# Experts stage of a decoder layer: results and row numbers in four buffers, each with its own semaphore, instead of two

## The chip, the core and the metric

The kernel runs on one core of one Trainium2 chip. The metric is the device time of one execution in microseconds (us), as the median of several runs.

## What is computed

One decoder layer over 32 batches of 100 tokens of width 256, all in fp32: self-attention (16 heads of 64), cross-attention to 361 context rows per batch (16 heads of 16), and a mixture of experts. Only the last part is touched. Its reference, cut down (`feats` is the layer-normed input of the stage, 3200 rows of 256; E is 8, the inner width is 1024):

```python
aff = feats @ centroids.T
eid = jnp.argmax(aff, axis=1)
xhat = (feats - mu) * jax.lax.rsqrt(var + EPS)
for e in range(E):
    mask = (eid == e).astype(feats.dtype)[:, None]
    h = xhat * gamma[e] + beta[e]
    y = feats + jax.nn.relu(h @ w1[e] + b1[e]) @ w2[e] + b2[e]
    alpha = jax.nn.sigmoid(feats @ centroids[e])[:, None]
    out = out + mask * (alpha * y + (1.0 - alpha) * feats)
x = x + out
```

Every token goes to one expert, so `out` plus the residual is, per row, `xf + alpha * (relu(h @ w1 + b1) @ w2 + b2)`, with `xf` the input row plus its normed features.

## The kernel before

Self-attention and cross-attention take about the first 1200 us of the program. During cross-attention each token's row is also written, sorted by expert, into the DRAM tensor `routed_rows` (`xs`), with the token's number as its 257th word. Then `experts` (L2002) works through 20 tiles, written out one after the other in the program, in the repeated pattern of `HALVES` = 2, 2, 1, 2, 1: a tile with 2 halves has 256 rows (a big tile, twelve of them), a tile with 1 half has 128 (a small tile, eight of them). The small tiles are tiles 2, 4, 7, 9, 12, 14, 17 and 19. Which expert and which rows belong to a tile is read from a table at run time (`expert_of`, `load_rows`).

What each engine does, in the order of its own program:

- SP loads, for tile j + 2, the rows (L1993, three buffers) and then 2 MB of weights `w1` and `w2` (L1998, L1999, three buffers). The rows wait for tile j - 1's `xf` (on POOL) and its `token` (on DVE, semaphore `token_ready`, L2072); the weights wait for the last `psd_y` of tile j - 1.
- TensorE multiplies `h_in` by `w1` into four banks `psd_h` (L2249: eight groups f = 0 to 7; in fp32 each group is four matmuls in the trace). Group f waits until group f - 4 has been copied out of its bank (`copied`, L2247). Then it multiplies `hid` by `w2` into `psd_y` (L2260: per half, 16 matmuls in the trace), and transposes the next tile's `xhat` in between (L2229).
- ScalarE copies groups 0, 2, 4, 6 and 7 to `hid` with bias and relu (L2143), then scales the next tile's transposed rows to `h_in` (L2129) and computes `ez` = exp(-z) (L2133).
- VectorE (DVE) copies groups 1, 3 and 5 to `hid` (L2201). Between group 1 and group 3 it takes the moments of the next tile (L2155, L2159), and after group 5 it runs `normalize(j + 1)` (`xhat` L2166, `feats` L2171) and `weigh(j + 1)`: the product with the centroid (L2179), its sum `z` (L2183), the row numbers `token` (L2185), then `ez` + 1 (L2187, after ScalarE's exp) and `alpha` (L2190). Only then comes tile j's own end: `y` = `psd_y` + bias (L2215) and `res` (L2219), for each half. All of it is one queue: what stands behind `token` in this order waits with it.
- GpSimd (POOL) runs `roots(j + 1)` (L2083 to L2087), then `finish(j - 1)`, which issues one indirect DMA per half that scatters `res` to the output rows that `token` names (L2102), then `residual(j + 1)` (`xf`, L2095).

`token` and `res` have two buffers each, j % 2, and so has the semaphore `scattered` that counts their scatters. So DVE waits before it overwrites them:

```python
reach(dve, scattered[j % 2], 16 * halves_until(j, 2))
dve.tensor_copy(token[:, j % 2, 0:nh], rows[:, j % 3, 0:nh, D]).then_inc(token_ready, 1)
```

Here, in `weigh(j)`, the scatters of tile j - 2 must have landed. The same wait stands a second time before `y` and `res` of tile j (L2211), where it has already been met.

Of the kernel before, what the change touches and what calls it, by code (L numbers as in the profile page):

```python
# [2001 lines left out]
def experts(nc, c, xs, w1, w2, out):  # L2002
# [4 lines left out]
    with ExitStack() as ctx:  # L2007
# [21 lines left out]
        ez = sb("ez", [128, 2])  # L2029
        alpha = sb("alpha", [128, 2, 2])  # L2030
        xf = sb("xf", [128, 2, 2, D])
        token = sb("token", [128, 2, 2], U32)
        h_in = sb("h_in", [128, 2, KD, T])
        hid = sb("hid", [128, NF, T])
        y = sb("y", [128, 2, D])
        res = sb("res", [128, 2, 2, D])

        ps_x = psum("psd_x", [128, KD * T])
        ps_h = [psum(f"psd_h{i}", [128, 512]) for i in range(4)]
# [10 lines left out]
        ez_ready = sem("ez_ready")  # L2050
        weight_steps = sem("weight_steps")
        xf_ready = sem("xf_ready")
        token_ready = sem("token_ready")
        turned = sem("turned4")
        h_in_ready = sem("h_in_ready")
        hid_filled = sem("hid_filled")
# [9 lines left out]
        @block.sync  # L2066
        def _(sp):
            load_rows(sp, c, 1, xs)
            sp.wait_ge(c.tiles_ready, 4)
            for j in range(TILES - 2):  # L2070
                reach(sp, xf_ready, j)
                reach(sp, token_ready, j)  # L2072
                load_rows(sp, c, j + 2, xs)
                reach(sp, y_filled, halves_until(j))
                load_weights(sp, c, j + 2, w1_sb[(j + 2) % 3], w2_sb[(j + 2) % 3], w1, w2)

        @block.gpsimd
        def _(pool):
            def roots(j):
                nh = HALVES[j]  # L2080
                pool.wait_ge(moment_steps, 2 * halves_until(j + 1))
                pool.sem_inc(pool_passed, 1)
                pool.tensor_scalar(var_eps[:, 0, 0:nh], mv[:, 0:nh, 1], 1.0 + EPS, EPS * EPS, ALU.mult, ALU.add  # L2083
                                   ).then_inc(root_steps, 1)
                pool.tensor_scalar(var_eps[:, 1, 0:nh], mv[:, 0:nh, 1], EPS, None, ALU.add).then_inc(root_steps, 1)
                pool.wait_ge(root_steps, 3 * j + 2)
                pool.tensor_tensor(rstd[:, :, 0:nh], var_eps[:, :, 0:nh],  # L2087
                                   c.minus_half[:, 0:2 * nh].rearrange("p (u t) -> p u t", u=2), ALU.pow
                                   ).then_inc(root_steps, 1)

            def residual(j):
                nh = HALVES[j]
                pool.wait_ge(normalised, 2 * j + 2)
                reach(pool, res_ready, halves_until(j - 1))
                pool.tensor_tensor(xf[:, j % 2, 0:nh], rows[:, j % 3, 0:nh, 0:D], feats[:, 0:nh], ALU.add  # L2095
                                   ).then_inc(xf_ready, 1)

            def finish(j):
                for t in range(HALVES[j]):
                    pool.wait_ge(res_ready, halves_until(j) + t + 1)  # L2100
                    pool.sem_inc(pool_passed, 1)
                    pool.indirect_dma_start(  # L2102
                        out=out, out_offset=bass.IndirectOffsetOnAxis(ap=token[:, j % 2, t:t + 1], axis=0),
                        in_=res[:, j % 2, t, :], in_offset=None, bounds_check=B * S - 1,
                        oob_is_err=False).then_inc(scattered[j % 2], 16)

            roots(0)
            residual(0)
            for j in range(TILES):
                if j + 1 < TILES:  # L2110
                    roots(j + 1)
                if j > 0:
                    finish(j - 1)
                if j + 1 < TILES:
                    residual(j + 1)
            finish(TILES - 1)
            for j in (TILES - 2, TILES - 1):
                pool.wait_ge(scattered[j % 2], 16 * halves_until(j + 2, 2))

        @block.scalar  # L2120
        def _(act):
# [26 lines left out]
        @block.vector  # L2148
        def _(dve):
            dve.wait_ge(c.tables, 16 * 5)  # L2150

            def moments(j):
                dve.wait_ge(rows_loaded[j % 3], 16 * (j // 3 + 1))
                for t in range(HALVES[j]):
                    dve.bn_stats(stats[:, t], rows[:, j % 3, t, 0:D]).then_inc(moment_steps, 1)  # L2155
                dve.wait_ge(moment_steps, halves_until(j) + halves_until(j + 1))
                dve.sem_inc(dve_passed, 1)
                for t in range(HALVES[j]):
                    dve.bn_aggr(mv[:, t], stats[:, t]).then_inc(moment_steps, 1)  # L2159

            def normalize(j):

                dve.wait_ge(root_steps, 3 * j + 3)
                reach(dve, turned, j)
                for t in range(HALVES[j]):
                    ins = dve.tensor_scalar(xhat[:, t], rows[:, j % 3, t, 0:D], mv[:, t, 0:1], rstd[:, 0, t:t + 1],  # L2166
                                            ALU.subtract, ALU.mult)
                ins.then_inc(normalised, 1)
                reach(dve, xf_ready, j)
                for t in range(HALVES[j]):  # L2170
                    ins = dve.tensor_scalar(feats[:, t], rows[:, j % 3, t, 0:D], mv[:, t, 0:1], rstd[:, 1, t:t + 1],  # L2171
                                            ALU.subtract, ALU.mult)
                ins.then_inc(normalised, 1)

            def weigh(j):
                nh, e = HALVES[j], expert_of(dve, c, j)
                dve.wait_ge(normalised, 2 * j + 2)
                dve.sem_inc(dve_passed, 1)
                dve.tensor_tensor(prod[:, 0:nh], feats[:, 0:nh], c.cen[:, bass.ds(e, 1), :].to_broadcast([128, nh, D]),  # L2179
                                  ALU.mult).then_inc(weight_steps, 1)  # L2180
                dve.wait_ge(weight_steps, 3 * j + 1)
                reach(dve, ez_ready, j)
                dve.tensor_reduce(z[:, 0:nh], prod[:, 0:nh], AX_X, ALU.add).then_inc(z_ready, 1)  # L2183
                reach(dve, scattered[j % 2], 16 * halves_until(j, 2))
                dve.tensor_copy(token[:, j % 2, 0:nh], rows[:, j % 3, 0:nh, D]).then_inc(token_ready, 1)  # L2185
                dve.wait_ge(ez_ready, j + 1)
                dve.tensor_scalar(ez[:, 0:nh], ez[:, 0:nh], 1.0, None, ALU.add).then_inc(weight_steps, 1)  # L2187
                dve.wait_ge(weight_steps, 3 * j + 2)
                reach(dve, res_ready, halves_until(j - 1))
                dve.reciprocal(alpha[:, j % 2, 0:nh], ez[:, 0:nh]).then_inc(weight_steps, 1)  # L2190

            moments(0)
            normalize(0)
            weigh(0)
            for j in range(TILES):
                nh, e = HALVES[j], expert_of(dve, c, j)
                for f in HID_DVE:
                    dve.wait_ge(hid_filled, NF * j + (f + 1))
                    if f == 1:
                        reach(dve, y_filled, halves_until(j))  # L2200
                    dve.tensor_scalar(hid[:, f, 0:UNIT * nh], ps_h[f % 4][:, 0:UNIT * nh], c.b1_sb[:, f, bass.ds(e, 1)],  # L2201
                                      0.0, ALU.add, ALU.max).then_inc(hid_dve, 1)
                    if f == 1 and j + 1 < TILES:
                        moments(j + 1)
                if j + 1 < TILES:
                    normalize(j + 1)
                    weigh(j + 1)
                e = expert_of(dve, c, j)
                dve.wait_ge(weight_steps, 3 * j + 3)
                dve.wait_ge(xf_ready, j + 1)  # L2210
                reach(dve, scattered[j % 2], 16 * halves_until(j, 2))  # L2211
                for t in range(nh):
                    n = halves_until(j) + t
                    dve.wait_ge(y_filled, n + 1)
                    dve.tensor_tensor(y[:, t], ps_y[n % 3][:, 0:D], c.b2_sb[:, bass.ds(e, 1), :].rearrange(  # L2215
                        "p o d -> p (o d)"), ALU.add).then_inc(y_ready, 1)
                for t in range(nh):
                    dve.wait_ge(y_ready, halves_until(j) + t + 1)
                    dve.scalar_tensor_tensor(out=res[:, j % 2, t], in0=y[:, t], scalar=alpha[:, j % 2, t:t + 1],  # L2219
                                             in1=xf[:, j % 2, t], op0=ALU.mult, op1=ALU.add).then_inc(res_ready, 1)  # L2220

        @block.tensor
# [44 lines left out]
def build(nc, ins, out):  # L2267
    c = Shared()
    with ExitStack() as ctx:
# [16 lines left out]
        c.tiles_ready = ctx.enter_context(nc.semaphore("tiles_ready"))  # L2286
        c.empty = sb("empty", [128, ROWW])
        c.xs_cleared = ctx.enter_context(nc.semaphore("xs_cleared"))
        c.scattered = [ctx.enter_context(nc.semaphore(f"scattered{p}")) for p in range(2)]
        c.act_passed = ctx.enter_context(nc.semaphore("act_passed"))  # L2290
        c.dve_passed = ctx.enter_context(nc.semaphore("dve_passed"))
        c.pool_passed = ctx.enter_context(nc.semaphore("pool_passed"))
# [61 lines left out]
```

## Time and profile before

| | |
|---|---|
| median of 3 runs | 1494.63 us (1489.18, 1494.63, 1497.31) |
| profiled execution, its own time | 1491.62 us |
| its span | 1489.4 us, so 2.2 us lie around it |
| TensorE busy | 1374.4 us (92%) |
| VectorE busy | 939.5 us (63%) |
| ScalarE busy | 759.9 us (51%) |
| GpSimd busy | 652.3 us (44%) |
| experts stage, first to last of TensorE's steady work | 1254.3 to 1482.2 us |

Busy shares are means over stages of the program with different limits. In the rows further on, PE is TensorE, ACT is ScalarE, POOL is GpSimd, and "idle before" is the time an engine stood still just before an instruction, with the instruction that ended it behind the arrow.

### The profile page before, as it was taken

Reading aid. Unit: us, or ns where it says so; the run is one execution under the profiler, and the core shown is the slowest. Engines: PE = TensorE matmul, PEld = TensorE weight load, DVE = VectorE, ACT = ScalarE, POOL = GpSimd, SP = SyncE. Lnnn points to the kernel's source line nnn. Section 1 sums busy time; section 2 is a strip of 40 time slices with the busy share of each in tenths; the row PEclk is TensorE's granted clock in tenths of the full one; section 3 lists DMA queues with packets and bytes.
Section 4 is the critical chain, followed back from the end, with each engine's and each line's share of the span. In section 5 each row is a group of like instructions: output and inputs, shape, how many; then the busy total and the mean of one; then the engine's idle time right before and its main releaser. Section 6 shows DMA issues by size and latency. Waiting matters only on the chain.

```text
span 1489.4 us, 39019 instructions
## 1 busy us (share of the span) xinstructions
PE 1374.4 (92%) x12161; PEld 1188.1 (80%) x12161; DVE 939.5 (63%) x2386; ACT 759.9 (51%) x1880; POOL 652.3 (44%) x1000
## 2 busy tenths in 40 slices
PE   6999999999999999869999999999999947999997
PEld 5888888887878787757888888888888836887886
DVE  6757574747484756446777777777777754555453
ACT  5747474646465655515665656566565522222222
POOL 5635344443526271722345555545555442333332
PEclk9999999999999999979999999999999978999999
DMA  6607161524344343547677667776676626655551
GB/s 203 145 1 172 25 151 43 130 64 111 83 90 104 76 118 68 130 135 193 186 187 199 189 174 195 193 191 182 185 193 188 181 70 213 214 202 189 201 198 69
DMA packets 181115, 217.42 MB, mean 146 GB/s; under 512 B 83486, under 2 KB 148933, under 8 KB 180774
## 3 DMA queue, kind: packets, MB, share of 16 engines
q1 hardware_dynamic: 176424, 209.60, 51.2%
q0 software_dynamic: 3584, 6.58, 1.4%
q8 instruction: 43, 0.70, 0.2%
q10 hardware_dynamic: 1024, 0.21, 0.1%
q14 instruction: 40, 0.33, 0.1%
HBM read 137.62 MB, written 79.43 MB: 146 GB/s over the span
## 4 chain that ended last, share of the span: by engine, by line
PE 44%; DVE 4%; DMA 3%; issue 3%; POOL 2%; DVEq 0%; SPq 0%; ACT 0%; POOLq 0%; ACTq 0%
PE psb_s L1769 7%; PE psd_y L2260 6%; PE psb_o L1792 5%; PE psb_t L1779 5%; PE psd_h L2249 5%; PE psb_p L62 4%; PE psb_p L63 3%; PE psb_p L64 3%; DMA out<-res,token 2%; PE psb_p L1732 2%; PE psb_f L1815 2%; DVE row_max L1488 1%; PE psb_f L1800 1%; PE psb_p L1827 1%; PE psb_f L1806 1%
## 5 line engine op out<-in xcount | busy, mean ns | idle before, releaser
L1488 DVE TENSOR_REDUCE row_max<-psb_s 100x1 f32<-100x361 f32 x512 | 265.5, 531 | 142.1 <-PE psb_s L1769 136.2
L1362 ACT ACTIVATE probs<-psb_t 121x400 f32<-121x400 f32 (+1 forms) x384 | 190.5, 508 | 87.6 <-PE psb_t L1779 81.4
L1769 PE MATMUL psb_s<-k,q 97*100 97x362 f32 x512 | 185.2, 364 | 14.1 <-DMA k<-packed_keys 5.4
L540 POOL TENSOR_TENSOR diag<-neg_ident,row_max 100x400 fp32r<-100x400 f32 x128 | 112.9, 903 | 168.8 <-DVE row_max L632 140.1
L1779 PE MATMUL psb_t<-q,k 98*121 98x200 f32 (+1 forms) x768 | 146.3, 273 | 1.7 <-ACT probs L1362 1.7
L1779 PEld LDWEIGHTS psb_t<-q,k 98*121 98x121 f32 (+1 forms) x768 | 125.3, 184 | 4.6 <-ACT probs L1362 2.4
L451 ACT ACTIVATE probs<-ps_t 100x400 f32<-100x400 f32 x128 | 57.5, 501 | 111.5 <-PE ps_t L787 111.5
L1769 PEld LDWEIGHTS psb_s<-k,q 97*100 97x100 f32 x512 | 85.8, 168 | 34.0 <-issue 20.7
L2143 ACT ACTIVATE hid<-psd_h,b_sb 128x256 f32<-128x256 f32 (+1 forms) x100 | 43.2, 432 | 121.0 <-PE psd_h L2249 120.9
L2249 PE MATMUL psd_h<-h_in,w_sb 128*128 128x256 f32 (+1 forms) x448 | 86.7, 350 | 8.4 <-DVE hid L2201 6.9
L1792 PE MATMUL psb_o<-probs,v_ext 121*32 121x100 f32 (+1 forms) x3072 | 92.7, 253 | 0.0
L526 POOL CAST o_hi<-stage 128x400 fp32r<-128x400 f32 x64 | 59.9, 936 | 69.5 <-ACT stage L461 33.4
L2249 PEld LDWEIGHTS psd_h<-h_in,w_sb 128*128 128x128 f32 x448 | 74.7, 194 | 19.4 <-DVE hid L2201 9.2
L306 ACT COPY q_t<-ps_p 64x200 f32<-64x200 f32 x112 | 57.1, 510 | 63.4 <-PE ps_p L64 62.5
L62 PE MATMUL ps_p<-x_lo,w_hi 128*128 128x400 f32 x224 | 82.1, 366 | 4.6 <-DVE q_t L306 0.2
L632 DVE TENSOR_REDUCE row_max<-ps_s 100x4 f32<-100x400 f32 x128 | 67.6, 571 | 28.6 <-PE ps_s L743 28.1
L461 ACT COPY stage<-ps_ot 64x200 f32<-64x200 f32 x256 | 81.8, 319 | 6.1 <-PE ps_ot L797 1.2
L528 POOL TENSOR_TENSOR o_lo<-stage,o_hi 128x400 fp32r<-128x400 f32 x64 | 81.8, 1277 | 5.1
L2260 PE MATMUL psd_y<-w_sb,hid 128*128 128x256 f32 x368 | 83.9, 379 | 0.0
L1792 PEld LDWEIGHTS psb_o<-probs,v_ext 121*32 121x32 f32 (+1 forms) x3072 | 64.4, 110 | 21.3 <-issue 16.9
L64 PE MATMUL ps_p<-x_hi,w_hi 128*128 128x400 f32 x224 | 77.2, 345 | 0.0
L63 PE MATMUL ps_p<-x_hi,w_lo 128*128 128x400 f32 x224 | 76.7, 342 | 0.0
(252 smaller groups left out, 3714.3 us busy)
## 6 DMA issues: line engine op xcount, KB each, us to landing
w_sb<-in_w SPq DMA_DIRECT2D x28, 1024.0 KB
routed_rows<-empty SPq DMA_DIRECT2D x7, 3855.0 KB, 19.6
packed_keys<-k_st SPq DMA_DIRECT2D x32, 724.0 KB, 4.2
k<-packed_keys SPq DMA_DIRECT2D x64, 362.0 KB
v_rows<-v_tok SPq DMA_DIRECT2D x32, 400.0 KB
v_ext<-v_rows SPq DMA_DIRECT2D x32, 400.0 KB
q<-packed_queries SPq DMA_DIRECT2D x64, 200.0 KB
w_third<-in_w SPq DMA_DIRECT2D x12, 1024.0 KB
```

Source lines behind the costliest of these rows:

```text
L62: pe.matmul(out, hi_l, lo_r, start=first, stop=False)
L63: pe.matmul(out, lo_l, hi_r, start=False, stop=False)
L64: return pe.matmul(out, hi_l, hi_r, start=False, stop=last)
L461: act.copy(*turned_part(r - 2, a, odd)).then_inc(ot_copied_act, 1)
L540: pool.tensor_tensor(diag[:, g % 2], c.neg_ident[0:S, 0:S].unsqueeze(1).to_broadcast([S, GH, S]), row_max[:, g // 2 % 2, g % 2].unsqueeze( ...
L1362: act.activation(probs[0:KT[kt], u % 2, kt], ps_t[i % 2][0:KT[kt], 0:4 * S], ACT.Exp, scale=HD2 ** -0.5).then_inc(probs_ready, 1)
L1488: dve.reduce_max(row_max[:, p, h:h + 1], ps_s[h % 2][0:S, 0:S2], AX_X).then_inc(max_ready, 1)
L1769: pe.matmul(ps_s[h % 2][0:S, 0:S2E], q2[0:97, p, u, g, S * a:S * (a + 1)], k2[0:97, p, u, g], start=True, stop=True).then_inc(scores_ready, 1)
L1779: ins = pe.matmul(ps_t[i % 2][0:n, 2 * S * g:2 * S * (g + 1)], k2[:, p, u, g, rows], q2[:, p, u, g], start=True, stop=True)
L1792: ins = pe.matmul(ps_o[32 * h:32 * (h + 1), S * u:S * (u + 1)], v_ext[0:n, p, kt, 4 * u + h, :], probs[0:n, u % 2, kt, S * h:S * (h + 1)], ...
L2249: ins = pe.matmul(ps_h[f % 4][:, 0:UNIT * nh], w1_sb[j % 3][:, k, 128 * f:128 * (f + 1)], h_in[:, j % 2, k, 0:UNIT * nh], start=(k == 0), ...
L2260: ins = pe.matmul(ps_y[n % 3][:, 0:D], hid[:, f, UNIT * t:UNIT * (t + 1)], w2_sb[j % 3][:, f, :], start=(f == 0), stop=(f == NF - 1))
```

## The change

`token` and `res` get four buffers, j % 4, and `scattered` becomes four semaphores, so that tile j waits for the scatters of tile j - 4. `token_ready` is gone: `token` now counts on `weight_steps`, which takes four steps per tile instead of three, and SP waits there for the same instruction as before. The end of the stage waits for the last four tiles' scatters instead of the last two. No instruction is added, taken away or moved on any engine; only what some of them wait for differs.

```diff
-        token = sb("token", [128, 2, 2], U32)
+        token = sb("token", [128, 4, 2], U32)
...
-        res = sb("res", [128, 2, 2, D])
+        res = sb("res", [128, 4, 2, D])
...
-        token_ready = sem("token_ready")
...
-                reach(sp, token_ready, j)
+                reach(sp, weight_steps, 4 * (j - 1) + 2)
...
-                        out=out, out_offset=bass.IndirectOffsetOnAxis(ap=token[:, j % 2, t:t + 1], axis=0),
-                        in_=res[:, j % 2, t, :], in_offset=None, bounds_check=B * S - 1,
-                        oob_is_err=False).then_inc(scattered[j % 2], 16)
+                        out=out, out_offset=bass.IndirectOffsetOnAxis(ap=token[:, j % 4, t:t + 1], axis=0),
+                        in_=res[:, j % 4, t, :], in_offset=None, bounds_check=B * S - 1,
+                        oob_is_err=False).then_inc(scattered[j % 4], 16)
...
-            for j in (TILES - 2, TILES - 1):
-                pool.wait_ge(scattered[j % 2], 16 * halves_until(j + 2, 2))
+            for j in range(TILES - 4, TILES):
+                pool.wait_ge(scattered[j % 4], 16 * halves_until(j + 4, 4))
...
-                dve.wait_ge(weight_steps, 3 * j + 1)
+                dve.wait_ge(weight_steps, 4 * j + 1)
                 reach(dve, ez_ready, j)
                 dve.tensor_reduce(z[:, 0:nh], prod[:, 0:nh], AX_X, ALU.add).then_inc(z_ready, 1)
-                reach(dve, scattered[j % 2], 16 * halves_until(j, 2))
-                dve.tensor_copy(token[:, j % 2, 0:nh], rows[:, j % 3, 0:nh, D]).then_inc(token_ready, 1)
+                reach(dve, scattered[j % 4], 16 * halves_until(j, 4))
+                dve.tensor_copy(token[:, j % 4, 0:nh], rows[:, j % 3, 0:nh, D]).then_inc(weight_steps, 1)
                 dve.wait_ge(ez_ready, j + 1)
                 dve.tensor_scalar(ez[:, 0:nh], ez[:, 0:nh], 1.0, None, ALU.add).then_inc(weight_steps, 1)
-                dve.wait_ge(weight_steps, 3 * j + 2)
+                dve.wait_ge(weight_steps, 4 * j + 3)
...
-                dve.wait_ge(weight_steps, 3 * j + 3)
+                dve.wait_ge(weight_steps, 4 * j + 4)
                 dve.wait_ge(xf_ready, j + 1)
-                reach(dve, scattered[j % 2], 16 * halves_until(j, 2))
+                reach(dve, scattered[j % 4], 16 * halves_until(j, 4))
...
-                    dve.scalar_tensor_tensor(out=res[:, j % 2, t], in0=y[:, t], scalar=alpha[:, j % 2, t:t + 1],
+                    dve.scalar_tensor_tensor(out=res[:, j % 4, t], in0=y[:, t], scalar=alpha[:, j % 2, t:t + 1],
...
-        c.scattered = [ctx.enter_context(nc.semaphore(f"scattered{p}")) for p in range(2)]
+        c.scattered = [ctx.enter_context(nc.semaphore(f"scattered{p}")) for p in range(4)]
```

## Rows read from the trace of the kernel before

**Rows 1.** The page, busy time, share of the span and instructions of each engine.
```profile
PE 1374.4 (92%) x12161; PEld 1188.1 (80%) x12161; DVE 939.5 (63%) x2386; ACT 759.9 (51%) x1880; POOL 652.3 (44%) x1000
```

**Rows 2.** Stretches: busy time by engine, granted TensorE clock, DMA share, GB/s.
```profile
750.00:810.00 60.00, 59.34 (x695) 51.33 (x695) 43.73 (x119) 36.12 (x97) 29.30 (x55) 1.00 0.68 180
1237.00:1254.30 17.30, 16.41 (x69) 14.16 (x70) 8.24 (x22) 4.44 (x11) 2.85 (x5) 0.85 0.40 138
1254.30:1482.20 227.90, 218.64 (x1145) 191.13 (x1143) 117.90 (x320) 59.91 (x149) 76.63 (x103) 1.00 0.55 186
```

**Rows 3.** TensorE's waits from 1254 to 1483 us: total, times, longest.
```profile
PE psd_h L2249 <- DVE hid L2201: 9.1, 7, 1.9
```

**Rows 4.** VectorE's longest waits, same stretch and columns.
```profile
DVE token L2185 <- DMA out<-res,token: 27.8, 15, 3.2
DVE ez L2187 <- ACT ez L2133: 19.4, 11, 2.9
```

**Rows 5.** TensorE in order of time: start, duration, operation, idle before, at tiles 1, 2, 3, 10.
```profile
1254.30 7.07 PE L2249 MATMUL psd_h<-h_in,w_sb 128*128 128x256 f32 x32
1261.20 3.62 PE L2260 MATMUL psd_y<-w_sb,hid 128*128 128x256 f32 x16
...
1268.33 3.95 PE L2249 MATMUL psd_h<-h_in,w_third 128*128 128x128 f32 x32
...
1276.13 4.48 PE L2249 MATMUL psd_h<-h_in,w_sb 128*128 128x256 f32 x20
1281.98 2.86 PE L2249 MATMUL psd_h<-h_in,w_sb 128*128 128x256 f32 x12 [1.38 <-DVE hid L2201]
1284.68 3.62 PE L2260 MATMUL psd_y<-w_sb,hid 128*128 128x256 f32 x16
...
1360.32 4.48 PE L2249 MATMUL psd_h<-h_in,w_sb 128*128 128x256 f32 x20
1366.66 2.86 PE L2249 MATMUL psd_h<-h_in,w_sb 128*128 128x256 f32 x12 [1.86 <-DVE hid L2201]
1369.36 3.62 PE L2260 MATMUL psd_y<-w_sb,hid 128*128 128x256 f32 x16
```

**Rows 6.** VectorE in order of time, from tile 3's weights to its first copy.
```profile
1275.55 0.69 DVE L2183 TENSOR_REDUCE z<-prod 128x2 f32<-128x512 f32 x1
1278.96 0.17 DVE L2185 CAST token<-stage 128x2 uint32<-128x2 f32 x1 [2.72 <-DMA out<-res,token]
1279.03 0.16 DVE L2187 TENSOR_SCALAR ez<-ez 128x2 f32<-128x2 f32 x1
1279.23 0.17 DVE L2190 RECIPROCAL alpha<-ez 128x2 f32<-128x2 f32 x1
1280.15 0.42 DVE L2215 TENSOR_TENSOR y<-psd_y,b_sb 128x256 f32<-128x256 f32 x1 [0.75 <-DVE alpha L2190]
1280.61 0.48 DVE L2219 SCALAR_TENSOR_TENSOR res<-y,alpha,xf 128x256 f32<-128x256 f32 x1
1281.45 0.48 DVE L2201 TENSOR_SCALAR hid<-psd_h,b_sb 128x256 f32<-128x256 f32 x1 [0.35 <-issue]
```

**Rows 7.** The chain of waits, start, duration, what.
```profile
1274.79 4.14 DMA out<-res,token
```

**Rows 8.** POOL in order of time, behind that transfer's issue.
```profile
1275.78 1.30 POOL L2095 TENSOR_TENSOR xf<-stage,feats 128x512 f32<-128x512 f32 x1
```

**Rows 9.** VectorE in order of time at tile 0, with no scatter to wait for.
```profile
1237.90 0.69 DVE L2183 TENSOR_REDUCE z<-prod 128x2 f32<-128x512 f32 x1
1238.50 0.16 DVE L2185 CAST token<-stage 128x2 uint32<-128x2 f32 x1
1238.86 0.17 DVE L2187 TENSOR_SCALAR ez<-ez 128x2 f32<-128x2 f32 x1 [0.20 <-ACT ez L2133]
```

**Rows 10.** ScalarE in order of time, tile 3's exponential.
```profile
1276.27 0.20 ACT L2133 ACTIVATE ez<-z 128x2 f32<-128x2 f32 x1 [0.47 <-DVE z L2183]
```

**Rows 11.** VectorE in order of time, the longest product with the centroid (tile 6).
```profile
1309.40 1.66 DVE L2179 TENSOR_TENSOR prod<-feats,cen 128x512 f32<-128x512 f32 x1 [0.24 <-DVE feats L2171]
```

## Prediction

> **What bounds the kernel now.** The page comes first: TensorE is busy 92% of the span [rows 1], so a change pays only where it shortens TensorE's work or one of its pauses. Second, the stretches: from 1254.3 to 1482.2 us, where tiles 1 to 19 run, TensorE is busy 218.64 of 227.90 us at a granted clock of 1.00 [rows 2]. That leaves 9.26 us of pause, the most visible prize in the part of the program that the diff touches. Third, who TensorE waited for there: one partner alone, VectorE's copy `hid`, 7 times, 9.1 us, at most 1.9 each [rows 3]. Fourth, who VectorE waited for: `token` for the scatters, 27.8 us in 15 waits, then `ez` for ScalarE, 19.4 us in 11 [rows 4]. So the 27.8 us are not what can be won. The question is how much of them reaches TensorE.
>
> The timeline at tile 3 shows how they do. Tile 2 is small, so TensorE is through it in 7.8 us (1268.33 to 1276.13) [rows 5]. VectorE has summed `z` at 1275.55 to 1276.24 and could write `token` at once. It does so at 1278.96 [rows 6], when the second scatter of tile 1, issued at 1274.79, has landed 4.14 us later [rows 7]. Behind `token` in VectorE's queue stand `ez`, `alpha`, tile 2's `y` and `res`, and only then group 1 of tile 3, at 1281.45 [rows 6]. TensorE needs that bank for group 5 and stops until 1281.98 [rows 5]. The same picture comes at every big tile that follows a small one: tiles 3, 5, 8, 10, 13, 15, 18. The other eight of the 15 waits are followed by a wait for `ez`, which comes from ScalarE and in the end from TensorE, so they are covered and worth nothing.
>
> **What the change removes.** Tile 1, big and behind a big tile, shows an undisturbed first half: from the first `psd_h` matmul to the first `psd_y` one, 1261.20 − 1254.30 = 6.90 us for 32 matmuls, 0.216 us each. Tile 3 needs 1284.68 − 1276.13 = 8.55 us, 1.65 more, although its listed pause is 1.38; tile 10 needs 1369.36 − 1360.32 = 9.04, 2.14 more, with 1.86 listed [rows 5]. So a stop costs about 0.27 us beyond the idle shown, as the pipeline refills. Seven stops: 9.1 + 7 × 0.27 = **11.0 us**.
>
> Does VectorE come early enough without the wait? Tile 0 has no scatter to wait for: `token` starts 0.60 us and `ez` + 1 starts 0.96 us after `z` starts [rows 9]. At tile 3 that puts `ez` + 1 at 1276.51, right behind ScalarE's exponential, which ends at 1276.47 [rows 10]. Before, it stood at 1279.03, so all behind it moves up by 2.52 us: `alpha` to 1276.71, `y` to 1277.63, `res` to 1278.09, group 1's copy to 1278.93. TensorE went on 0.53 us after that copy started (1281.45 to 1281.98), so bank 1 is free at 1279.46. TensorE arrives for group 5 at 1276.13 + 20 × 0.216 = 1280.44. The slack is 1.0 us, and the stop is gone, not shortened. The start of `z` lies 0.58 us ahead of TensorE's first `psd_h` matmul here; that sequence hangs on TensorE's own work, so the other six tiles should have the same slack. Group 3's copy follows with only the next tile's moments in between, is needed two groups later, and moves up with it.
>
> **What it adds.** Nothing on any queue: every engine issues the same instructions in the same order. The new wait of tile j is for tile j − 4's scatters. They are issued while tile j − 3 runs, about two tiles before (one small and one big, 7.8 + 14.0 us, at the least), and take some 4 us [rows 7]: 0. SP waits for the same `token` instruction under another semaphore's name, and its row loads start up to 2.8 us earlier; they were never late after tile 0: 0. POOL's last wait names four tiles instead of two, and the two older ones landed long before the last scatter: 0. The same bytes move in 11 us less, which lifts the DMA share from 0.55 to 0.55 × 227.9 / 216.9 = 0.58, while 0.68 stood beside undisturbed matmuls earlier [rows 2]: 0. The cover of all these zeros is TensorE's work of 7.8 us or more per tile. If it went, the next late thing would be group 1's copy, 1.0 us away, and then POOL's path to `xhat` in the small tiles.
>
> The cost that no row settles is how VectorE fares when its small operations run beside POOL's `xf`. At tile 3 `xf` runs from 1275.78 to 1277.08 [rows 8], and `token`, `ez` and `alpha` would now fall inside it; before, they came after it. The lower bound is nothing: `z`, 0.69 us here, runs into `xf` and takes the same 0.69 as at tile 0 [rows 6, 9]. The upper bound from rows is the product with the centroid at tile 6, 1.66 us beside `xf` [rows 11] against the 0.69 that `z` takes for as many elements, so 0.97 us on the path, just inside the slack of 1.0. I take nothing, since `z` is the nearest row in time and place; even the upper bound leaves the stop at about zero. What could shift beyond is kept in a rival.
>
> The Trainium skill ("SBUF — State Buffer", "SBUF: two separate sides") has a rule against this change: VectorE and GpSimd share a pair of ports as an exclusive lock, held for the whole instruction, and a VectorE copy, cast or tensor_scalar in a two-port mode is blocked until GpSimd is through. By that rule `ez` + 1 would wait for `xf`'s end at 1277.08 instead of starting at 1276.51; the slack would be 0.4 us instead of 1.0, and the sum still 11.0. No run here shows `token` or `ez` beside `xf`.
>
> **The sum.** Against the profiled execution's own time: 1491.62 − 11.0 = 1480.6 us. That execution lies 3.0 us below the median shown; the mean of all four times is 1493.2, and I take that as the base: 1493.2 − 11.0 = **1482.1 us**, 0.74% less. About 0.5% (7.5 us) is what a measurement of this kernel can tell from no change.
>
> **The rivals.**
>
> *Part of the stop stays.* `xf` and the small operations hold each other up by more than the slack, say 1.8 us instead of 0 to 0.97. For it: at tile 6 `xf` and the product overlap and one of them took over twice its time. Against it: `z` did not suffer. It would bring back 0.8 of idle at each of the seven tiles, with the refill 7 × (0.8 + 0.12) = 6.4 us: a gain of 4.6 us, 1488.6 us. Chance 0.06.
>
> *The change does not do what it says, or the wait is another's.* The releaser of `token` is inferred from semaphores; were it VectorE's own queue or the row buffer, the four buffers would free nothing. For it: nothing but that inference. Against it: the wait ends with the landing each time, and tile 0, which has no scatter to wait for, shows none. 1493.2 us. Chance 0.05.
>
> *Slower: TensorE's clock.* Without pauses TensorE would work about 217 us on end in this stage. If the granted clock then fell from its upper level (2.4 GHz) to its lower (1.2 GHz), each us of matmuls would cost two. The place is the tail of the stage; the deciding point is 11.0 us of matmuls at the lower level, less than one big tile (14.0 us). Two big tiles would give −11.0 + 28.0 = +17.0, 1510.2 us. For it: the clock was 0.85 in tile 0. Against it: that followed a long idle at the stage's opening, and from 750 to 810 us TensorE was busy 59.34 of 60 us at 1.00 [rows 2]. Chance 0.03.
>
> **How the numbers follow.** The forecast has 0.86. Within it I give 0.08 to a measurement that comes out within 0.5%, because 11.0 us is only 3.5 above that bound and runs of one kernel spread over 8 us. Faster: 0.86 − 0.08 = 0.78. Same: 0.08 + 0.06 + 0.05 = 0.19. Slower: 0.03. The range takes the run spread around the forecast, 1489.18 − 11.0 = 1478.2 at the fast end with 1.5 us to spare, so 1476.7, and reaches up over the partial case to 1489.0. The no-change case and the slow one, 0.08 together, lie outside.
>
> **What would show it.** In the new profile TensorE's waits for `hid` in this stage are gone, and each of the seven segments from `psd_h` to `psd_y` is 6.9 us. The wait of `token` for the DMA is gone in all 15 places; `ez` takes over part of it in the eight covered ones, so VectorE's wait for ScalarE grows by several us, at no cost. Group 1's copy at tile 3 starts 2.8 us after TensorE's first `psd_h` matmul instead of 5.3. The stretch from tile 1 to tile 19 shrinks from 227.9 to 217 us with TensorE busy 99% or more of it, clock 1.00. I would be wrong if stops of 0.3 us or more remain at these tiles, if a wait for POOL (`xhat`, `xf`) appears in their place, or if the clock row falls.

## The result and the profile after

The changed kernel takes 1483.57 us (median of 6 runs, 1481.74 to 1484.26), the kernel before, run beside it, 1495.12 us. The ratio is 0.9926, 95% interval 0.9909 to 0.9942: 0.74% or 11.0 us less by the ratio, and 11.55 us between the two medians.

The page's line on engines, which answers to [rows 1]:

```profile
PE 1375.4 (93%) x12161; PEld 1191.5 (80%) x12161; DVE 943.5 (64%) x2386; ACT 760.0 (51%) x1880; POOL 651.0 (44%) x1000
```

TensorE does the same instructions in the same busy time; VectorE is busy 4.0 us longer, which comes up again below. The stretch from tile 1's first `psd_h` to the end of tile 19's `psd_y` answers to the third line of [rows 2]:

```profile
1256.24:1472.94 216.70, 216.69 (x1145) 191.71 (x1143) 122.05 (x320) 59.90 (x149) 76.20 (x103) 1.00 0.58 196
```

It lasted 227.85 us before (1254.30 to 1482.15) and lasts 216.70 us now: 11.15 us less. TensorE is busy 216.69 of them, at a granted clock of 1.00. In this stretch the view of waits, which had [rows 3] for TensorE, has no line for TensorE's matmuls at all. The span fell from 1489.4 to 1480.3 us, 9.1; the other 2 us are the stages ahead, where this execution reached the stage 1.9 us later (1256.24 against 1254.30).

TensorE in order of time at tiles 2, 3 and 10 (start, duration, operation), against [rows 5]:

```profile
1270.28 3.95 PE L2248 MATMUL psd_h<-h_in,w_third 128*128 128x128 f32 x32
...
1278.07 7.07 PE L2248 MATMUL psd_h<-h_in,w_sb 128*128 128x256 f32 x32
1284.98 3.62 PE L2259 MATMUL psd_y<-w_sb,hid 128*128 128x256 f32 x16
...
1357.76 7.07 PE L2248 MATMUL psd_h<-h_in,w_sb 128*128 128x256 f32 x32
1364.66 3.62 PE L2259 MATMUL psd_y<-w_sb,hid 128*128 128x256 f32 x16
```

Tile 3's 32 matmuls are one piece again, 1284.98 − 1278.07 = 6.91 us instead of 8.55, and tile 10's 6.90 instead of 9.04. Over the seven tiles the segments lost 10.98 us of the stretch's 11.15; most of the rest is tile 7, small, whose segment took 3.77 us instead of 3.91.

VectorE's waits in the stretch (total, times, longest), against [rows 4]:

```profile
DVE ez L2186 <- ACT ez L2132: 32.0, 11, 3.8
DVE hid L2200 <- PE psd_h L2248: 15.0, 23, 1.2
```

The wait of `token` for the scatters, 27.8 us in 15 times, is gone. The wait for ScalarE's exponential grew from 19.4 to 32.0 us at no cost. Of these 12.6 us, 11.3 stand at the eight tiles where `token` had been covered, and there 9.2 us of its wait are gone: mostly the same idle time under another name.

VectorE in order of time at tile 3, against [rows 6], and POOL's `xf` beside it:

```profile
1277.49 0.69 DVE L2182 TENSOR_REDUCE z<-prod 128x2 f32<-128x512 f32 x1
1278.09 0.95 DVE L2184 CAST token<-stage 128x2 uint32<-128x2 f32 x1
1278.96 0.15 DVE L2186 TENSOR_SCALAR ez<-ez 128x2 f32<-128x2 f32 x1
1279.15 0.17 DVE L2189 RECIPROCAL alpha<-ez 128x2 f32<-128x2 f32 x1
1280.00 0.42 DVE L2214 TENSOR_TENSOR y<-psd_y,b_sb 128x256 f32<-128x256 f32 x1 [0.69 <-DVE alpha L2189]
1280.46 0.48 DVE L2218 SCALAR_TENSOR_TENSOR res<-y,alpha,xf 128x256 f32<-128x256 f32 x1
1281.30 0.48 DVE L2200 TENSOR_SCALAR hid<-psd_h,b_sb 128x256 f32<-128x256 f32 x1 [0.35 <-issue]
```

```profile
1277.72 1.29 POOL L2094 TENSOR_TENSOR xf<-stage,feats 128x512 f32<-128x512 f32 x1
```

`token` now follows `z` without a gap, but lasts 0.95 us instead of 0.16: it ends at 1279.04, when `xf` ends at 1279.01. Group 1's copy starts 1281.30 − 1278.07 = 3.23 us after TensorE's first `psd_h` matmul, against 5.32 before and the 2.80 that the prediction worked out.

A way to read all the runs below follows from this. Call that distance d: from TensorE's first `psd_h` matmul of a tile to VectorE's copy of group 1. [rows 5] and [rows 6] suggest that the copy may start up to d = 3.78 us without harm: TensorE arrives for group 5 after 20 matmuls, 4.31 us, and it went on 0.53 us after the copy started. The lengths of the segments put this limit a little lower, at 3.68 us (table below, under "How much slack there is"), and by it the slack is 3.68 − d. Before, d was 5.32 at tile 3 and the slack −1.64; now it is +0.45. Over the seven tiles d now lies between 3.08 and 3.30, so the slack is 0.38 to 0.60 us.

### The profile page after: what moved, and what is told of

Same layout as the page of the kernel before. It is cut to its first block, busy times and chain, and to the rows that moved or that the text cites. A ratio compares the mean times of both kernels' runs of the same rounds, so it can differ in the third digit from the quotient of the medians.

```text
span 1480.3 us, 39018 instructions
## 1 busy us (share of the span) xinstructions
PE 1375.4 (93%) x12161; PEld 1191.5 (80%) x12161; DVE 943.5 (64%) x2386; ACT 760.0 (51%) x1880; POOL 651.0 (44%) x1000
## 4 chain that ended last, share of the span: by engine, by line
PE 46%; DVE 4%; issue 2%; DMA 2%; POOL 1%; SPq 1%; ACT 0%; DVEq 0%; ACTq 0%; POOLq 0%
PE psd_h L2248 8%; PE psd_y L2259 7%; PE psb_s L1769 6%; PE psb_t L1779 4%; PE psb_o L1792 4%; PE psb_p L62 4%; PE psb_p L63 3%; PE psb_p L64 3%; DVE row_max L1488 2%; PE psb_p L1732 2%; PE psb_f L1815 2%; DVE k_st L1471 1%; PE psb_f L1800 1%; DMA k<-packed_keys 1%; PE psb_p L1827 1%
```

## The experiments

A profile's span also holds the stages ahead, which differ from one execution to the next (tile 1 began anywhere from 1254 to 1268 us). So for mechanisms I compare the stretch from tile 1 to tile 19 in each profile, and the timed ratio to the kernel before for the whole.

**Which of the buffers matters.** Two kernels take the change apart. The first keeps two buffers of results and two semaphores:

```diff
-        res = sb("res", [128, 4, 2, D])
+        res = sb("res", [128, 2, 2, D])
...
-                reach(dve, scattered[j % 4], 16 * halves_until(j, 4))
                 dve.tensor_copy(token[:, j % 4, 0:nh], rows[:, j % 3, 0:nh, D]).then_inc(weight_steps, 1)
...
-                reach(dve, scattered[j % 4], 16 * halves_until(j, 4))
+                reach(dve, scattered[j % 2], 16 * halves_until(j, 2))
```

> Four buffers of row numbers, but two of results and two semaphores as before; the row numbers wait for nothing of their own, since VectorE waits for the scatters of tile j - 4 before it writes tile j - 2's results. Theory A (the stop comes from the row numbers' wait alone, because it stands ahead of y, res and group 1's copy): all of the gain, ratio about 0.993 to the kernel before, no wait of TensorE for hid, span near 1480 us. Rival B (the wait for two result buffers, met today only because the other wait comes first, becomes the new stop): VectorE waits for the scatter at y, up to 2.7 us at the seven places less the 2 us that pass between the two instructions, so stops of 0.3 to 1 us stay and the ratio is 0.995 to 1.0.

Measured: ratio 0.9908 (0.9882 to 0.9934), stretch 216.83 us, no wait of TensorE for `hid`. Theory A holds: the wait in front of `y` is met when VectorE gets there. The reason is in the program. `token` of tile j + 1 is written while tile j runs, ahead of tile j's own `res`. So with two buffers it waits for the scatters of tile j − 1, which have only just been issued, while `res` of tile j waits for those of tile j − 2, a whole tile older. The expected span of about 1480 us did not come: this execution spent longer in the stages ahead, reached tile 1 at 1265.65 us and had a span of 1489.8.

The second has four buffers of results only:

```diff
-        res = sb("res", [128, 2, 2, D])
+        res = sb("res", [128, 4, 2, D])
...
-                        in_=res[:, j % 2, t, :], in_offset=None, bounds_check=B * S - 1,
+                        in_=res[:, j % 4, t, :], in_offset=None, bounds_check=B * S - 1,
```

> Four buffers of results, but two of row numbers, with the waits of the kernel before. Theory A: nothing moves, ratio 1.000 within 0.002, the wait of token for the scatter 27 to 28 us in 15 times, TensorE waits for hid 7 times, 9 us. Rival B: a gain of a few us.

Measured: ratio 0.9998 (0.9980 to 1.0016), stretch 226.99 us. TensorE's and VectorE's waits from 1225 us on:

```profile
PE psd_h L2249 <- DVE hid L2201: 8.3, 7, 2.1
```

```profile
DVE token L2185 <- DMA out<-res,token: 27.1, 15, 3.5
```

Nothing moved. This edit changes no wait, only where `res` lies, so by itself it says little; together with the first kernel it says that the whole gain comes from `token`, 8 bytes per partition and buffer, and none from the 4 KB per partition that `res` took besides.

**How many buffers.** Both with three instead of four:

```diff
-        token = sb("token", [128, 4, 2], U32)
+        token = sb("token", [128, 3, 2], U32)
...
-        res = sb("res", [128, 4, 2, D])
+        res = sb("res", [128, 3, 2, D])
...
-                reach(dve, scattered[j % 4], 16 * halves_until(j, 4))
+                reach(dve, scattered[j % 3], 16 * halves_until(j, 3))
```

> Three buffers of both and three semaphores instead of four. The row numbers of tile j wait for tile j - 3's scatters, which land a whole tile (7.8 us or more) before. Theory A: same time as with four, ratio 0.993, no wait for the DMA at token. Rival (scatters run late enough that three are short): waits of token for the DMA of more than 0.2 us in some tiles and a ratio nearer 1.

Measured: ratio 0.9920 (0.9892 to 0.9947), stretch 216.72 us, no wait of `token` for the DMA. Three do what four do: with three, `token` too waits for scatters that are a tile older.

**Or no buffer more.** The kernel before, with the wait and the cast moved behind `res` in VectorE's queue (`number` holds the two lines that `weigh` loses; `number(0)` follows `weigh(0)`):

```diff
                 dve.tensor_reduce(z[:, 0:nh], prod[:, 0:nh], AX_X, ALU.add).then_inc(z_ready, 1)
-                reach(dve, scattered[j % 2], 16 * halves_until(j, 2))
-                dve.tensor_copy(token[:, j % 2, 0:nh], rows[:, j % 3, 0:nh, D]).then_inc(token_ready, 1)
...
                                              in1=xf[:, j % 2, t], op0=ALU.mult, op1=ALU.add).then_inc(res_ready, 1)
+                if j + 1 < TILES:
+                    number(j + 1)
```

> The kernel before with two buffers of each; the row numbers and their wait are moved from the weights of tile j + 1 to behind the results of tile j, so that y, res no longer stand behind the wait, but group 1's copy still does. Theory A (place in the queue is what counts; group 1's copy may start up to 3.78 us after the first psd_h matmul): at tile 3 the scatter lands 2.8 us after that matmul, so the copy starts at about 3.3 us and TensorE doesn't stop; at tile 10, where the landing came latest (3.3 us), the copy starts near 3.8 us, at the edge. All or nearly all of the gain: ratio 0.993 to 0.994. Rival (buffers are needed, the order doesn't matter): ratio 0.998 to 1.0, TensorE's seven waits stay.

Measured: ratio 0.9926 (0.9899 to 0.9953), stretch 217.76 us, 1.0 more than with four buffers. One of TensorE's seven waits is left in the view, at tile 10, the one expected at the edge:

```profile
1368.28 2.86 PE L2255 MATMUL psd_h<-h_in,w_sb 128*128 128x256 f32 x12 [0.23 <-DVE hid L2205]
```

VectorE there, with the wait for the scatter now behind `res`:

```profile
1365.76 0.49 DVE L2223 SCALAR_TENSOR_TENSOR res<-y,alpha,xf 128x256 f32<-128x256 f32 x1
1366.91 0.17 DVE L2193 CAST token<-stage 128x2 uint32<-128x2 f32 x1 [0.66 <-DMA out<-res,token]
1367.74 0.48 DVE L2205 TENSOR_SCALAR hid<-psd_h,b_sb 128x256 f32<-128x256 f32 x1 [0.67 <-PE psd_h L2255]
```

`psd_h` began at 1363.57, so d = 4.17, past 3.68 by 0.49; the segment is 0.49 us longer than 6.91, and 0.23 of that is shown as idle. The copy came later than the expected 3.8, since 0.66 us pass between the end of the cast and the copy. At tiles 8, 13 and 18 d was 3.77, 3.79 and 3.88, and the segments are 0.10, 0.11 and 0.20 us longer with no idle shown at all. Tile 18, whose segment is 1465.26 − 1458.15 = 7.11 us:

```profile
1458.15 7.27 PE L2255 MATMUL psd_h<-h_in,w_sb 128*128 128x256 f32 x32
1465.26 3.62 PE L2266 MATMUL psd_y<-w_sb,hid 128*128 128x256 f32 x16
```

Together these four are 0.90 of the 1.06 us that the stretch is longer. It was the order of VectorE's queue that turned a late scatter into a stop. The extra buffers are one cure, another order nearly as good a one.

**Why `token` lasts 0.95 us.** The changed kernel with the cast ahead of the product (the counts that wait on it shift by one):

```diff
+                reach(dve, scattered[j % 4], 16 * halves_until(j, 4))
+                dve.tensor_copy(token[:, j % 4, 0:nh], rows[:, j % 3, 0:nh, D]).then_inc(weight_steps, 1)
                 dve.tensor_tensor(prod[:, 0:nh], feats[:, 0:nh], c.cen[:, bass.ds(e, 1), :].to_broadcast([128, nh, D]),
                                   ALU.mult).then_inc(weight_steps, 1)
...
                 dve.tensor_reduce(z[:, 0:nh], prod[:, 0:nh], AX_X, ALU.add).then_inc(z_ready, 1)
-                reach(dve, scattered[j % 4], 16 * halves_until(j, 4))
-                dve.tensor_copy(token[:, j % 4, 0:nh], rows[:, j % 3, 0:nh, D]).then_inc(weight_steps, 1)
```

> The changed kernel with the row numbers written ahead of the product with the centroid, so that they no longer fall beside POOL's xf at the small tiles. Theory A (lock: what VectorE does as a copy, cast or tensor_scalar beside xf is held until xf ends): the 20 casts take 0.14 to 0.17 us each, but at small tiles ez + 1 takes their place, lasts 0.6 us or more instead of 0.15 and ends with xf; group 1's copy at tile 3 still starts 3.1 to 3.3 us after the first psd_h matmul. Rival B (only the conversion to an integer is slow there): ez + 1 lasts 0.16 us and group 1's copy starts 2.8 us after. The time is that of the changed kernel either way, ratio to the kernel before 0.992 to 0.993, since TensorE doesn't wait for it.

Measured: ratio 0.9925 (0.9902 to 0.9948), stretch 216.70 us. VectorE at tile 3, and POOL:

```profile
1278.08 0.17 DVE L2179 CAST token<-stage 128x2 uint32<-128x2 f32 x1
1278.20 0.69 DVE L2180 TENSOR_TENSOR prod<-feats,cen 128x512 f32<-128x512 f32 x1
1278.93 0.69 DVE L2184 TENSOR_REDUCE z<-prod 128x2 f32<-128x512 f32 x1
1279.88 0.58 DVE L2186 TENSOR_SCALAR ez<-ez 128x2 f32<-128x2 f32 x1 [0.27 <-ACT ez L2132]
```

```profile
1279.13 1.29 POOL L2094 TENSOR_TENSOR xf<-stage,feats 128x512 f32<-128x512 f32 x1
```

The cast here takes 0.17 us, and `ez` + 1, 0.15 us in the changed kernel, takes 0.58 and ends at 1280.46 with `xf` (1280.42). Over the seven tiles `ez` + 1 takes 0.39 to 0.58 us, a little under the 0.6 expected. d is 1282.65 − 1279.49 = 3.16, close to the 3.23 with the cast behind: theory A at this place. One part of the expectation failed. Over all 20 tiles the casts took 8.2 us, as much as in the changed kernel, and not 0.14 to 0.17 us each. At the five other big tiles, 0, 1, 6, 11 and 16, POOL starts `xf` before VectorE reaches the early cast, and there it is now the cast that is held, for 1.04 to 1.23 us. At tile 6, VectorE and then POOL:

```profile
1309.51 1.23 DVE L2179 CAST token<-stage 128x2 uint32<-128x2 f32 x1
```

```profile
1309.45 1.26 POOL L2094 TENSOR_TENSOR xf<-stage,feats 128x512 f32<-128x512 f32 x1 [0.18 <-DVE feats L2170]
```

In the changed kernel, as in the one before [rows 11], it is the product that is held at these tiles. At tile 6 of the kernel before, `xf` had started 0.15 us ahead of it:

```profile
1309.25 1.25 POOL L2095 TENSOR_TENSOR xf<-stage,feats 128x512 f32<-128x512 f32 x1 [0.19 <-DVE feats L2171]
```

The product took 1.66 us and ended 0.56 after `xf`. With the cast ahead, it starts once `xf` is through and takes 0.68:

```profile
1310.65 0.68 DVE L2180 TENSOR_TENSOR prod<-feats,cen 128x512 f32<-128x512 f32 x1
```

So whatever of these comes second beside `xf` pays. Moving an operation away from `xf` at one kind of tile put it beside `xf` at another.

**How much slack there is.** The changed kernel with one, then three sums between `y` and `res` of the seven small tiles that a big one follows; their results go nowhere (shown with three):

```diff
+                if nh == 1 and j + 1 < TILES:
+                    for n in range(3):
+                        dve.tensor_reduce(spare[:, n, 0:2], prod[:, 0:2], AX_X, ALU.add)
```

> The changed kernel with one more sum of 512 elements (0.60 us from start to start; its result goes nowhere) on VectorE between y and res of the seven small tiles that a big one follows. Theory A (slack of 0.5 to 0.6 us behind the held cast, then each further us costs seven): group 1's copy starts near 3.8 to 3.9 us, stops of 0 to 0.2 us, cost 0 to 2.5 us in all, ratio to the kernel before 0.993 to 0.995. Rival (slack of 1.0 us, as if the cast cost nothing): no listed stop at any of the seven, ratio 0.9925 or less. Rival (any delay of VectorE there is paid in full): 4.2 us, 0.996.

Measured: ratio 0.9930 (0.9902 to 0.9957), stretch 216.84 us, no stop. But this doesn't measure the slack: group 1's copy hardly moved, d = 3.26 instead of the expected 3.8 to 3.9. VectorE at tile 3:

```profile
1292.25 0.68 DVE L2219 TENSOR_REDUCE spare<-prod 128x2 f32<-128x512 f32 x1
1292.85 0.47 DVE L2222 SCALAR_TENSOR_TENSOR res<-y,alpha,xf 128x256 f32<-128x256 f32 x1
1293.24 0.48 DVE L2201 TENSOR_SCALAR hid<-psd_h,b_sb 128x256 f32<-128x256 f32 x1
```

The sum takes up 0.60 us of the queue, yet the copy moved by 0.03. The copy now starts 0.39 us after `res` instead of 0.84, and the 0.35 us of idle in that gap is gone; the sum starts 0.34 after `y` where `res` started 0.46 after it. The profile names no cause for that idle time ("issue"). The program has VectorE read the tile's expert number from a table at this place, and the reading that this work now goes on while the sum runs fits, but is not shown.

> The same with three such sums, 1.8 us. Theory A: group 1's copy starts 5.0 to 5.1 us after the first psd_h matmul (3.23 + 1.8), bank 1 is free 0.53 us later, TensorE arrives at 4.31: seven listed stops of 0.9 to 1.2 us and, with the refill, 7 x 1.3 = 9 us on top of the changed kernel's time, ratio to the kernel before 0.998 to 1.0. Rival (the gain came from elsewhere, for instance from DMA traffic or the row loads): the gain stays, ratio 0.993.

Measured: ratio 0.9967 (0.9949 to 0.9985), stretch 222.32 us, 5.6 more than the changed kernel. VectorE and TensorE at tile 3:

```profile
1279.51 1.86 DVE L2219 TENSOR_REDUCE spare<-prod 128x2 f32<-128x512 f32 x3
1281.29 0.47 DVE L2222 SCALAR_TENSOR_TENSOR res<-y,alpha,xf 128x256 f32<-128x256 f32 x1
1281.68 0.48 DVE L2201 TENSOR_SCALAR hid<-psd_h,b_sb 128x256 f32<-128x256 f32 x1
```

```profile
1277.24 4.48 PE L2252 MATMUL psd_h<-h_in,w_sb 128*128 128x256 f32 x20
1282.21 2.86 PE L2252 MATMUL psd_h<-h_in,w_sb 128*128 128x256 f32 x12 [0.49 <-DVE hid L2201]
1284.90 3.62 PE L2263 MATMUL psd_y<-w_sb,hid 128*128 128x256 f32 x16
```

d is 1281.68 − 1277.24 = 4.44, not the expected 5.0, since the first of the sums is all but free, as above. The segment takes 7.66 us instead of 6.91: 0.75 more. The seven segments together are 5.3 of the measured 5.6 us longer. The cost is less than the 9 us expected, and the ratio lies below the 0.998 expected. All seven stops are back, 0.38 to 0.55 us each (and an eighth, 0.18 us, in a small tile), with VectorE's delay alone and four buffers of everything. So the size was off, and the relation is a simple one. d and the segment from the first `psd_h` matmul to the first `psd_y` one, read from the traces of five kernels ("late cast" is the one with the cast behind `res`); an undisturbed segment is 6.91 us:

| kernel, tile | d | segment | over 6.91 | d less that |
|---|---|---|---|---|
| changed, 3 | 3.23 | 6.91 | 0 | |
| late cast, 3 | 3.55 | 6.91 | 0 | |
| late cast, 8 | 3.77 | 7.01 | 0.10 | 3.67 |
| late cast, 10 | 4.17 | 7.40 | 0.49 | 3.68 |
| three sums, 3 | 4.44 | 7.66 | 0.75 | 3.69 |
| before, 5 | 4.71 | 7.94 | 1.03 | 3.68 |
| before, 3 | 5.32 | 8.55 | 1.64 | 3.68 |
| before, 10 | 5.81 | 9.04 | 2.13 | 3.68 |
| `res` alone, 10 | 6.04 | 9.27 | 2.36 | 3.68 |

These traces have 25 segments at the seven tiles that were longer than 6.91 us, and in all of them the last column is 3.67 to 3.69. TensorE lost what the copy came later than 3.68 us, and nothing more. The idle time shown is 0.26 or 0.27 us less than that loss at every one of them that is listed. By [rows 5], 0.17 of it is that 20 matmuls are listed as 4.48 us long where the next one could start after 4.31, and 0.11 that the 12 matmuls behind the stop take 2.70 us to the first `psd_y` one where 12 × 0.216 is 2.59. A stop that costs less than that isn't listed.

**What is next.** With the stage full, TensorE's longest idle time near it is its opening, 18.2 us, and the chain of waits there runs through SP's issues and the landing of tile 0's rows. One edit ahead of the stage:

```diff
             sp.wait_ge(c.tiles_ready, 2)
-            load_weights(sp, c, 0, c.w1_sb[:, 0], c.w2_sb[:, 0], moe["w1"], moe["w2"])
             for p in range(2):
                 sp.wait_ge(routed[p], 16 * (B // 2))
             load_rows(sp, c, 0, xs)
+            load_weights(sp, c, 0, c.w1_sb[:, 0], c.w2_sb[:, 0], moe["w1"], moe["w2"])
```

> The changed kernel with one more edit ahead of the stage: SP issues the rows of tile 0 before the weights of tile 0 instead of behind them. In the changed kernel the chain runs from SP's weights (issued 1224.36) through the rows (issued 1226.56, landing 6.95 us later) to the first moments, and TensorE is idle 18.2 us. Theory: the rows are issued about 1.5 to 2 us earlier and don't queue behind 2 MB of weights, landing in 3 to 4 us; TensorE's first transpose comes 4 to 6 us earlier, ratio to the kernel before 0.988 to 0.990. Rival (the weights become the last to arrive, or the rows are slow by themselves): idle time stays at 16 us or more, or a wait for w_sb appears, ratio 0.992.

The wait that opens the stage, of the changed kernel and then of this one:

```profile
PE psd_x L2228 <- DVE xhat L2165: 18.2, 1, 18.2
```

```profile
PE psd_x L2228 <- DVE xhat L2165: 14.0, 1, 14.0
```

4.2 us of idle are gone, and no wait for the weights appears; the stretch stays at 216.71 us. The rows are issued 5.5 us after TensorE's idle time begins instead of 7.4, and tile 0's first moments start 4.7 us behind that issue instead of 7.0. The timed ratio was 0.9913 (0.9884 to 0.9943), above the expected 0.988 to 0.990 and too wide to tell from the changed kernel, so both ran again side by side:

> The changed kernel once more, unaltered, as the partner of the next run on the same chip. Theory: ratio to the kernel before 0.9926 within 0.002.

> Tile 0's rows ahead of its weights, once more beside the changed kernel. The one look showed TensorE's idle time at the stage's opening at 14.0 instead of 18.2 us. Theory: those 4.2 us are on the path, so the ratio to the kernel before is 0.9926 - 0.0028 = 0.990 and the median lies 3 to 5 us below that of the changed kernel. Rival (they are given back, for instance in tile 0, whose weights now arrive later, or lost in the spread of the stages ahead): the medians agree within 1.5 us.

Measured: the changed kernel 0.9915 (0.9897 to 0.9933), 1482.71 us; with the rows first 0.9886 (0.9867 to 0.9906), 1481.02 us. The ratios lie 0.0029 apart, as the 4.2 us would give, but the intervals overlap, and the medians differ by only 1.7 us, where 3 to 5 were expected and the rival had at most 1.5. The traces say more. From the start of that idle time to the last instruction the changed kernel took 261.10 and 260.95 us in its two traces, and with the rows first 257.31 and 257.18: 3.8 us less each time, where the traces of other kernels with no stop of TensorE's lie between 260.8 and 261.7. So the stage is shown to be shorter by nearly all of it. That the whole kernel gains it is likely and not shown: the start of that idle time, set by the stages ahead, lies anywhere from 1217 to 1231 us in these traces.

## Why the prediction was right, and where it wasn't

The forecast was 1482.1 us and a gain of 11.0; measured were 1483.57 and a ratio of 0.9926 where 0.74% less, 0.9926, was said. The 1.5 us between the two times come mostly from the base: it was taken as 1493.2, and the kernel before, beside the changed one, took 1495.12, while the gain between the medians was half a us larger than forecast. (1493.2 − 11.0 is 1482.2; nothing hangs on the tenth.)

- **What bounds the kernel, and seven stops of 9.1 us that cost 0.27 more each.** Right. The seven segments lost 10.98 us, and with three sums put in, 0.49 us of idle again cost 0.75, that is 0.26 more. "As the pipeline refills" is not shown: most of the 0.27 is how the profile lists idle time, and TensorE lost just what the copy came late.
- **The other eight waits of `token` are covered.** Right. `ez` took their place; its wait grew by 12.6 us, where "several us" was said.
- **Group 1's copy comes in time.** Right in its sign, wrong in size. The step that failed is "I take nothing, since `z` is the nearest row": the small operations do pay beside `xf`. The term of 0 to 0.97 us measured 0.43 (d 3.23 instead of 2.80), and the slack was 0.45 us, not 1.0. `z` could not show this: it starts at 1275.55, 0.23 us before `xf` [rows 6, 8], and what pays is the operation that starts second. The product at tile 6, taken as the upper bound, started 0.15 us after its `xf` and was the row to judge by. That the term at its full 0.97 would leave "the stop at about zero" is right only just: by the limit of 3.68 the slack without any hold is 0.88, and it would have cost about 0.1 us at each of the seven tiles. The slack covered the mistake, so the time came out in spite of it.
- **The rule of the Trainium skill** ("SBUF — State Buffer", "SBUF: two separate sides"): first the rows: `token`, 0.95 us, ended 0.03 after `xf`, and in its place `ez` + 1, 0.58 us, ended 0.04 after it. By that rule, a copy, cast or tensor_scalar in a two-port mode that comes second waits for the whole of GpSimd's instruction. The trace agrees here. By it d would have been 2.80 + 0.57 = 3.37, an estimate, and it was 3.23. The same page ("Who interferes with whom") says that a sum is never held on this chip. The trace agrees: at tile 4 of the changed kernel `z` started 0.37 us after `xf` and took 0.42, as at tile 2, where `xf` had ended before it.

```profile
1285.39 0.82 POOL L2094 TENSOR_TENSOR xf<-stage,feats 128x256 f32<-128x256 f32 x1
```

```profile
1285.76 0.42 DVE L2182 TENSOR_REDUCE z<-prod 128x1 f32<-128x256 f32 x1
```

- **What the change adds: nothing.** Right. There is no new wait on any engine; the DMA share rose to 0.58, as worked out. One number in this part is off without effect: `token`'s longest wait was 3.2 us [rows 4], so the row loads could start up to 3.2 us earlier, not 2.8.
- **The rivals.** "Part of the stop stays" named the true mechanism, the hold beside `xf`, and failed on its price: it would have needed more than the slack, and took 0.43. The 0.8 us in its price is how late the copy comes, not idle time, so 0.12 beside it and 0.27 in the sum are no contradiction: by the table, 0.8 past 3.78 is a loss of 0.9. "The wait is another's" fell with the kernel that has four buffers of `token` alone: the wait and TensorE's stops went together. The slower case fell with the clock of 1.00 beside 216.69 us of work on end.
- **What was not asked.** The prediction took the four buffers as one thing. The runs split them: `res` did nothing, and three buffers, or two with the cast moved, do nearly the same.

## What to carry to other kernels

A wait costs what stands behind it in its queue, not what it lasts: 27.8 us of waiting were worth 11 here, all from the seven places where the copy that frees a bank for TensorE stood behind it. Before buying buffers, ask which of the tensors that share a semaphore is waited for first, and whether that wait can stand later in the queue: moving two lines gave all but 1 us of what two more buffers of everything gave. Then size the slack that is left, here 0.38 to 0.60 us, since every further us of lateness costs TensorE one, at each of the seven tiles. And take the size from the lengths of segments: the idle time listed is 0.26 us short at each stop and shows the smallest ones not at all.

## What the runs showed of the hardware

- A cast of two numbers per partition lasts 0.77 to 0.95 us instead of 0.16 when it starts while GpSimd runs a two-input elementwise operation of 1.10 to 1.30 us, and ends with it (1279.04 and 1279.01 at tile 3). A tensor_scalar of the same size does the same, 0.58 instead of 0.15, and a two-input product of 512 elements takes 1.66 instead of 0.70. The casts took 7.9 us in the stretch instead of 2.9. VectorE's busy time rose by 4.0 and not 5.0, because it counts the time in which two instructions overlap only once.
- A cast of one number per partition showed no such hold. At tile 9 of the changed kernel it started 0.71 us after `xf`, took 0.14 and ended 0.06 before it, and the same is seen at this tile in all eight traces where the cast falls beside `xf`; GpSimd's times are rough, so this rests on its 0.14 us and on the repetition.

```profile
1343.40 0.91 POOL L2094 TENSOR_TENSOR xf<-stage,feats 128x256 f32<-128x256 f32 x1
```

```profile
1344.11 0.14 DVE L2184 CAST token<-stage 128x1 uint32<-128x1 f32 x1
```

- The 0.35 us that VectorE stood idle before group 1's copy can be filled: 0.60 us of extra work ahead of it moved the copy by only 0.03 us.
- TensorE lost in each of 25 stopped segments what VectorE's copy came later than 3.68 us, to 0.01 us; the idle time listed is 0.26 us less. Its granted clock over the stretch was 1.00 in every trace, with seven stops or with none.
